# Attention of a first layer: one set of scores with a row-maximum bias, probabilities transposed by DMA, value products in bursts

## What is computed

```python
xn = _layernorm(x, axis=-1)
q = (xn @ Wq)  # 32 heads of 16;  k, v = xn @ Wk, xn @ Wv  # 8 heads of 16, each used by 4 q heads
attn = jnp.einsum('bhqd,bhkd->bhqk', q, k) * scale          # scale = 1/sqrt(16), float16
attn = jax.nn.softmax(attn, axis=-1).astype(jnp.float16)
out = jnp.einsum('bhqk,bhkd->bhqd', attn, v)
s = out @ Wo
g = _silu(_L0_ffn_ref(xn, ...))     # Hadamard transforms, up, gate, down
x = x + s * g                       # then the second layer
```

## Time and profile before

| | us |
|---|---|
| median of the runs | 1365.99 |
| lowest, highest of 3 runs | 1365.13, 1367.12 |
| span of the profiled execution | 1361.7 |
| of it, busy: PE / DVE / ACT / POOL | 1315.0 / 1063.5 / 737.4 / 528.7 |
| row maxima, L621, 512 of them | 329.1 |
| exponentials, L936, 512 of them | 277.1 |
| second scores, L1132, 512 of them | 99.7 |

### The profile page before, as it was taken

How to read it: one execution, slowest core, us unless ns; L and a number is a source line. 1 busy time by engine, 2 the same in 40 slices (tenths; PEclk the granted TensorE clock), 3 DMA queues, 4 the chain that set the end, 5 groups by cost and what they waited for, 6 DMA issues and landing times. The chain is left out here.

```text
span 1361.7 us, 24113 instructions
## 1 busy us (share of the span) xinstructions
PE 1315.0 (97%) x8866; PEld 640.7 (47%) x8866; DVE 1063.5 (78%) x1855; ACT 737.4 (54%) x1307; POOL 528.7 (39%) x434
## 2 busy tenths in 40 slices
PE   5888999999999999999999999999999999999998
PEld 2333333333333333333344546855486555855475
DVE  7888978778877887788884985778776976868846
ACT  5675666556655666556657552455334652355431
POOL 3499953012211221112222763247431762328431
PEclk9998999999999999999999999999999999999999
DMA  6520000010000000000254024002311024001121
GB/s 232 190 81 8 7 9 3 15 41 14 9 17 32 24 7 7 24 30 15 87 196 184 20 52 82 25 24 60 51 44 40 8 71 82 17 32 43 34 46 47
DMA packets 80468, 68.50 MB, mean 50 GB/s; under 512 B 46080, under 2 KB 67296, under 8 KB 77792
## 3 DMA queue, kind: packets, MB, share of 16 engines
q1 hardware_dynamic: 67936, 65.39, 15.5%
q10 hardware_dynamic: 12416, 1.57, 1.1%
HBM read 44.87 MB, written 17.87 MB: 46 GB/s over the span
## 5 line engine op out<-in xcount | busy, mean ns | idle before, releaser
L621 DVE TENSOR_REDUCE mS<-vpair 128x1 f16<-128x512 f32 x512 | 329.1, 685 | 111.6 <-PE vpair L1125 109.5
L936 ACT ACTIVATE probs<-bank 128x512 f16<-128x512 f32 x512 | 277.1, 594 | 163.0 <-PE bank L1132 162.8
L1179 PE MATMUL bank<-rows,both 128*128 128x512 f16 x1024 | 243.0, 380 | 0.4 <-DVE th L650 0.3
L436 POOL TENSOR_TENSOR h<-th,h 128x512 f16<-128x512 f32 x61 | 71.4, 1171 | 213.2 <-ACT h L907 213.2
L1179 PEld LDWEIGHTS bank<-rows,both 128*128 128x128 f16 x1024 | 91.3, 98 | 121.2 <-issue 13.9
L2257 PE MATMUL bank<-rows,both 128*128 128x512 f16 x512 | 118.6, 382 | 0.0
L1125 PE MATMUL vpair<-qk 32*128 32x512 f16 x512 | 100.3, 387 | 13.1 <-DVE mS L621 7.7
L2273 PE MATMUL bank<-both,hid 128*128 128x512 f16 x512 | 111.2, 379 | 0.0
L2241 PE MATMUL bank<-rows,both 128*128 128x512 f16 (+1 forms) x456 | 104.0, 379 | 0.9 <-PEq L160 0.9
L1132 PE MATMUL bank<-qv,qk 32*128 32x512 f16 x512 | 99.7, 386 | 0.0
L1193 PE MATMUL bank<-dn,h 128*128 128x512 f16 x256 | 98.0, 383 | 0.0
(11 more groups left out here) (363 smaller groups left out, 2654.1 us busy)
## 6 DMA issues: line engine op xcount, KB each, us to landing
h<-in_ug SPq DMA_DIRECT2D x8, 1024.0 KB, 5.5
lt_scratch<-big SPq DMA_DIRECT2D x16, 384.0 KB, 2.7
dn<-in_down SPq DMA_DIRECT2D x2, 2048.0 KB, 11.1
x_scratch<-th SPq DMA_DIRECT2D x16, 256.0 KB, 2.2
res<-x_scratch SPq DMA_DIRECT2D x16, 256.0 KB, 4.3
out_x<-res SPq DMA_DIRECT2D x16, 256.0 KB, 2.0
both<-in_w SPq DMA_DIRECT2D x2, 1548.0 KB, 10.4
t_scratch<-tok SPq DMA_DIRECT2D x16, 192.0 KB, 2.1
```

What stands on the lines that cost most here:

```text
L436: pool.tensor_tensor(h16(ft, 1), row32, h16(ft, 0), ALU.subtract).then_inc(S["row_lo"], 1)
L621: v.tensor_reduce(mS[:, u % 2, qt, 32 * j + DH:32 * j + DH + 1], SA[n % 2][:, :], AX.X, ALU.max).then_inc(S["max_done"], 1)
L936: a.activation(probs[:, n % (2 * G), :], SB[n % 2][:, :], ACT.Exp, scale=float(DH) ** -0.5).then_inc(S["p_ready"], 1)
L1179: mm = pe.matmul(GB[n % 2][:, :], w[:, kt, col:col + P], xnb(b, kt), start=r == 0, stop=r == 2 * KT - 1)
```

## The change

Scores are made once, with queries on the partitions, four tiles (four heads of one row tile) at a time into four banks `SC_`, in every second step (`scores`). The row maximum is negated and stays a column in float32 (`top_n`); the exponential takes it as bias and reads the same bank, so the scale goes into q's eviction. The probabilities of a row tile, 128 x 2048, lie in one of three buffers (`TAKEN`). SyncE transposes them by a DMA through the crossbar into `probsT`, keys on the partitions (`turn_probs`, one per two steps, 128 in all), once the four exponentials are there and, since `probsT` is single, once the unit before has been weighed. `weigh` makes a unit's 16 value products in one burst at the third step of the next unit (`PV_STEP`), when all its transposes have landed. `turn_maxima`, `q_aug`, `score_b`, `mS`, `qB` and `onecol` go; GpSimd clears k's padding. On VectorE four maxima stand together in even steps with `up_mul` ahead of them, and `chunk_max` moves a step earlier. Turning back to tokens, division and `to_features` stand 7, 7 and 6 steps earlier.

```diff
+TAKEN = 3
+PV_STEP, TOKEN_STEP, DIVIDE_STEP, TURN_BACK = 2, 3, 4, 6
-        SA, SB, OB, GB, MISC = bank[0:2], bank[2:4], bank[4], bank[5:7], bank[7]
+        SC_, OB, GB, MISC = bank[0:4], bank[4], bank[5:7], bank[7]
...
+        top_n = sb("top_n", [P, 2 * SC], F32)
+        probs = sb("probs", [P, TAKEN, G * T], F16)
+        probsT = sb("probsT", [P, SC, T], F16)
...
+            def turn_probs(n):
+                u, qt = divmod(n, TT)
+                sp.wait_ge(S["p_ready"], G * (n + 1))
+                if u:
+                    sp.wait_ge(S["pv_done"], u)
+                sp.dma_start_transpose(probsT[:, :, qt * P:(qt + 1) * P], probs[:, n % TAKEN, :]).then_inc(S[f"pt_in{n % TAKEN}"], 16)
...
             for t in range(TEND):
                 b, m = t // BSTEPS - 1, t % BSTEPS
+                if t % 2 == 0 and 0 <= t // 2 - 1 < NU * TT:
+                    turn_probs(t // 2 - 1)
...
-            pool.memset(mS[:, :, :, :], 0.0).then_inc(S["init"], 1)
+            pool.memset(ks[:, :, :], 0.0).then_inc(S["slots_set"], 1)
...
             def row_max(n):
+                v.wait_ge(S["s_ps"], n + 1)
+                i = n % (2 * SC)
+                v.tensor_reduce(top_n[:, i:i + 1], SC_[n % G][:, :], AX.X, ALU.max, negate=True).then_inc(S["max_done"], 1)
...
-                if t < NU * STEPS:
-                    row_max(2 * t)
-                    row_max(2 * t + 1)
...
+                if t > FFN_STEP + 1 and (t - 2) // BSTEPS < B and (t - 2) % BSTEPS >= FFN_STEP and t % 2 == 0:
+                    up_mul((t - 2) // BSTEPS, ((t - 2) % BSTEPS - FFN_STEP) // 2)
+                if t < NU * STEPS and t % 2 == 0:
+                    for j in range(G):
+                        row_max(2 * t + j)
...
             def exps(n):
+                a.wait_ge(S["max_done"], n + 1)
+                k, j = divmod(n, G)
+                if j == 0 and k >= TAKEN:
+                    a.wait_ge(S[f"pt_in{k % TAKEN}"], 16 * (k // TAKEN))
+                i = n % (2 * SC)
+                a.activation(probs[:, k % TAKEN, j * T:(j + 1) * T], SC_[j][:, :], ACT.Exp,
+                             bias=top_n[:, i:i + 1]).then_inc(S["p_ready"], 1)
...
+            def scores(n):
+                u, qt = divmod(n, TT)
+                if qt == 0:
                     pe.wait_ge(S[f"heads_in{u % SLOTS}"], 128 * (u // SLOTS + 1))
+                if n:
+                    pe.wait_ge(S["p_ready"], G * n)
+                for j in range(G):
+                    pe.matmul(SC_[j][:, :], qs[32 * j:32 * j + 32, u % SLOTS, qt * P:(qt + 1) * P],
+                              ks[32 * j:32 * j + 32, u % SLOTS, :], start=True, stop=True).then_inc(S["s_ps"], 1)
+
+            def weigh(u):
+                b, g = divmod(u, NKV)
+                for i in range(TAKEN):
+                    pe.wait_ge(S[f"pt_in{i}"], 16 * ((TT * (u + 1) - 1 - i) // TAKEN + 1))
...
+                for kt in range(TT):
+                    for j in range(G):
+                        mm = pe.matmul(OB[32 * j:32 * j + 32, :], vaug[:, b % 2, kt, g, :], probsT[:, TT * j + kt, :],
+                                       start=kt == 0, stop=kt == TT - 1)
...
-                if t < NU * STEPS + LAG:
-                    four_scores(t)
-                if t % STEPS == 0 and 0 < t <= NU * STEPS:
-                    turn_maxima(t // STEPS - 1)
+                if t < NU * STEPS and t % 2 == 0:
+                    scores(t // 2)
+                if t % STEPS == PV_STEP and 0 <= t // STEPS - 1 < NU:
+                    weigh(t // STEPS - 1)
```

More of the change, by code:

```diff
@@ L101, in misc_order @@
         b, m = t // BSTEPS, t % BSTEPS
-        if t % STEPS == 0 and 0 < t <= NU * STEPS:
-            order.append(("mT", t // STEPS - 1))
         if t in TURN_STEP:
@@ L800, in _ @@
                     inverse_deviations(3)
-                if r == 0 and 0 <= p < NCH:
-                    chunk_max(p)
-                    if p == NCH - 1:
-                        bound_inputs()
+                if r == 3 and 0 <= p + 1 < NCH:
+                    chunk_max(p + 1)
+                if r == 0 and p == NCH - 1:
+                    bound_inputs()
                 if t == 29:
@@ L979, in _ @@
             deviations(2)
-            a.wait_ge(S["init"], 4)
+            a.wait_ge(S["init"], 3)
             evict_v(0)
@@ L1111, in project_o @@
                 mm.then_inc(S["mb_full"], 1)
-            def turn_maxima(u):
-                pe.wait_ge(S["mb_took"], MB["mT", u])
-                pe.wait_ge(S["max_done"], (u + 1) * SC)
-                bk = MISC[:, :].bitcast(F16)
-                for qt in range(TT):
-                    mm = pe.transpose(bk[:, qt * P:(qt + 1) * P], mS[:, u % 2, qt, :], ident[:, :])
-                mm.then_inc(S["mb_full"], 1)
-            def score_a(n):
-                u, i = divmod(n, SC)
-                qt, j = divmod(i, G)
-                pe.matmul(SA[n % 2][:, :], qs[32 * j:32 * j + 32, u % SLOTS, qt * P:(qt + 1) * P],
-                          ks[32 * j:32 * j + 32, u % SLOTS, :], start=True, stop=True).then_inc(S["sa_ps"], 1)
@@ L1157, in weigh @@
+            def weigh(u):
                 b, g = divmod(u, NKV)
-                pe.wait_ge(S["p_ready"], G * w + G)
-                if kt == 0 and u:
+                for i in range(TAKEN):
+                    pe.wait_ge(S[f"pt_in{i}"], 16 * ((TT * (u + 1) - 1 - i) // TAKEN + 1))
+                if u:
                     pe.wait_ge(S["o_free"], u)
-                if kt == 0 and g == 0:
+                if g == 0:
                     pe.wait_ge(S["mb_took"], MB["v", b] + 1)
-                for j in range(G):
-                    mm = pe.matmul(OB[32 * j:32 * j + 32, :], vaug[:, b % 2, kt, g, :], probs[:, (G * w + j) % (2 * G), :],
-                                   start=kt == 0, stop=kt == TT - 1)
+                for kt in range(TT):
+                    for j in range(G):
+                        mm = pe.matmul(OB[32 * j:32 * j + 32, :], vaug[:, b % 2, kt, g, :], probsT[:, TT * j + kt, :],
+                                       start=kt == 0, stop=kt == TT - 1)
@@ L2614, in host_layout @@
     o["nhad"] = c(-had.astype(np.float32))
-    one = np.zeros((P, 1), np.float32)
-    one[DH::32] = 1.0
-    o["onecol"] = one
     return o
```

113 lines of the change are left out of this document (28 added, 85 removed).

## The result

| | before | after |
|---|---|---|
| median of the runs, us | 1366.55 | 1482.68 |
| lowest, highest | 1365.13, 1368.22 | 1479.72, 1485.11 |
| ratio, with its 95% interval | | 1.0858 (1.0842 to 1.0874) |
| span of the profiled execution | 1361.7 | 1477.9 |

The kernel became 8.6% slower, where 1375 us (+0.7%) was forecast. The span grew by 116.2 us. I cut both spans at the starts of scores in the timeline, at t = 0, 32, 64 and then each 32 steps. "To scores" is the time to the first scores.

A forecast was written before the change was run, and what follows sets the result against it. The bound was to go from TensorE to the chain of scores, maxima and exponentials. Span 1361.7 + 10.2 + 0.4 - 4 = 1368.3, medians 4.3 higher, plus 2.4 for start loads and x1 transfers: 1375 us (1355 to 1400); range 1340 to 1490.

The forecast's parts named there:

- The wait at the burst: TensorE waits for a unit's fourth transpose: 1.8 us, four times per down half (7.2 us); nothing in feed-forward halves.
- The formula of the wait: Down half: fourth transpose 1.8 us late, plus 4.0 landing and 0.1, less 4.1 until TensorE asks: 1.8 us.
- The issue of a transpose: SyncE's queue: 0.6 us per transpose, as for a plain DMA; 4.7 us if issued by blocks of 16 partitions.
- The halves without waits: First layer's double steps summed without transpose waits: down half 64.4 us (68.2 before), feed-forward half 81.3 (81.2 before).
- The exponential with a column bias: ScalarE's exponentials in the new loop, priced at 0.594 us each as in the kernel before.
- Tanh in the feed-forward chain: ScalarE's high half (0.63 us) and tanh (0.67) stand between exponential pairs, making the plain double step 4.7 us.
- Rival 2: Faster: transposes land in 3.0 us, issue 0.33, tanh perhaps outside the feed-forward loop; 1350 us (1335 to 1360), chance 0.31.
- The start: Steps t < 32: no change, 8 us either way, the same work but for its order.
- The end: After t = 256 nine steps lose their second scores, 0.33 + 0.1 us each: -4 us.
- Rival 1: SyncE's queue is the bound: issue by blocks, 4.7 us, gives 1570 us (1480 at 3.9); TensorE's clock falls; chance 0.22.
- Rivals 3 and 4: 3: transposes write 32 B pieces, over 2500 us, chance 0.03. 4: four scores don't overlap, 1375 to 1385, chance 0.02.

The follow-up runs named there:

- e4: The changed kernel without its 128 transposes and the waits on them, value products reading a constant tile; 1378.62 us, ratio 1.0099.
- e5: The changed kernel with each transpose replaced by a plain DMA of the same 512 KB in pieces of 256 B; 1461.03 us (one run).
- e7: The changed kernel with twelve extra, unused products on TensorE ahead of the burst's wait for the transposes; 1470.77 us, ratio 1.0772.
- e1: The changed kernel with a unit's eight head loads issued behind its fourth transpose, k's projection six steps later; 1388.71 us, ratio 1.0170.
- e8: e4 with the exponentials also taking no bias; 1361.48 us, ratio 0.9969.
- e9: e1 with the value burst one step later and the rows' high half ahead of a double step's first two exponentials; 1364.56 us, ratio 0.9990.
- e12: e9 with a block's four exponentials together at the even step for all t; 1417.72 us, ratio 1.0387.
- e11: e9 with a block's four exponentials together at the even step for t < 32 only; 1371.91 us, ratio 1.0046.
- e10: e9 with the next layer's first four loads issued ahead of the very last transpose; 1372.78 us, ratio 1.0053.

## Why the prediction was wrong

**The wait at the burst and what follows it (the step that failed).** The sum had this wait at 4 x 1.8 us in a down half, at nothing in a feed-forward half ("costs nothing"), and no price for the clock behind it: 21.6 us in all. With e4 as the kernel without transposes, the halves from t = 64 on show (us; the waits are the idle time just ahead of the bursts):

| | after | e4 | more | of it waits | rest | forecast |
|---|---|---|---|---|---|---|
| three down halves | 256.0 | 198.1 | 57.9 | 39.1 | 18.8 | 21.6 |
| three feed-forward halves | 278.4 | 238.9 | 39.5 | 25.1 | 14.4 | 0 |

So the term was 97 us and not 21.6. The mean wait is 3.3 us in a down half and 2.1 in a feed-forward half; the feed-forward halves, forecast at nothing, are the largest single miss. These 76 us are most of the 107 by which the forecast was short; the start and the end, below, are the others.

**The formula of the wait** was right: issue + loads + landing + 0.1, less two double steps. With what the trace shows for the burst at 455.74 it gives 1.93 + 5.7 + 4.33 + 0.1 - 7.9 - 0.33 = 3.8 us, measured 3.60; I had 1.8. Of the 2.0 more, 1.3 are the issue, 0.8 the eight head loads (5.7 for 4.93), 0.3 the landing, less 0.4 since the double steps are longer. In a feed-forward half the same terms give about 2 us, measured 2.31: the margin there was 0.3 us, and a margin as small as that was no reason to put the term at nothing.

**The issue of a transpose** is the input that was furthest off. I took 0.6 us, "since every plain DMA of whatever size is 0.33 to 0.6", and kept 0.33 to 1.2 for the range. It is 1.93. The rows of before had no transpose, and the evidence used was of another kind of DMA; even there 0.33 to 0.6 held for medians only (one load of 1 MB took 1.26). The 4.7 that I named as a rival bounded it from above, and a value between the two was the honest choice. But it is not the whole step: e5, with an issue of 0.65, still takes 1461 us (one run), 86 over the forecast.

**The clock behind the wait.** I had the fall of the clock in rows 7 and charged it to the first rival only. My own forecast had TensorE idle for 1.8 us in 12 bursts with no such charge. What the clock took is read in three ways: 1.2 us per burst of a down half on average by e7, 36.9 us of TensorE's busy time between the changed kernel and e1, and the rest of the table, 33.2, which holds whatever else differs. It does not fall behind every wait: a burst at 522.23 waited for 2.86 us, and the 4.3 us behind it were granted 1.00.

**The halves without waits: right in size.** 64.4 and 81.3 summed, 64.6 and 81.7 measured in e4 (the first down half, with 68.9, and the last feed-forward half, with 75.5, differ, as they did before). But the agreement hides the next error: the exponentials in these sums were too short, and other terms too long by as much (e8, with exponentials of 0.60, has 63.3 and 79.2).

**The exponential with a column bias.** 594 ns was taken from rows 4 for an instruction that got a new operand; it is 687 to 690. That is 17 us over the kernel (e8).

**Tanh in the feed-forward chain.** Rival 2 had it that plain double steps could be 4.4 us if something slipped out of the loop; they are 4.73 in the changed kernel, and 4.2 in e9, by the high half and not by tanh (e12 shows what becomes of tanh outside).

**The start.** "0, 8 us either way" for t < 32; it is +11.6, and +8.8 more for t = 32 to 63. By the first 32 steps: without transposes 112.9, also without bias 108.9, before 105.9. So 4.6 are the transposes and 4.0 the bias; the 3.0 left may be the order of four scores at a time, but no run isolates it. For the second stretch, transposes 0, bias 2.5, and the high half's place most of the rest (97.9 in e9). Why e9's first 32 steps are still 8.4 longer stays open in its parts; putting the pairs together makes it longer (e11).

**The end.** -4 was forecast, it is +8.3. I had counted nine steps without second scores and not what else starts there. The next layer's loads stand behind the last transpose in SyncE's queue: they start 785.74 - 777.5 = 8.2 us after the last scores, where before it was 671.9 - 669.6 = 2.3. In e4, without transposes, it is 684.3 - 680.3 = 4.0, and its end is still 6.3 over before's. So the queue explains a part, and what makes the rest was not isolated.

**Rival 1** ends up at the measured time (1480 at an issue of 3.9 us) by a wrong mechanism. It said that the queue is the bound from 2.9 us on; the issue is 1.93, the queue is not the bound (e1), and the loss is a place in the queue and the clock. Its note on the clock was right. Without that rival's width the range would have ended far below the time: that 1340 to 1490 holds 1482.68 is luck.

**Rivals 3 and 4** fell. The queue has 334032 packets where it had 67936: 2079 more per transpose, so pieces of 256 B and not of 32. And the four scores overlap: the two pairs start 0.01 us apart.

In sum: of the 116 us, e4 puts the transposes' part at 104, or up to 109 without the late first scores of e4; 94 of them went with the place of the fourth one (e1). What they cost in e1 all the same, 10 to 15 us, was not taken apart.

## What to carry to other kernels

Before a DMA is put into a full queue, list for each one what stands ahead of it in that queue and when the consumer asks for it; one late entry behind eight small loads cost 94 us here, and moving the loads behind it gave them back. A term that comes out at nothing by a small margin (0.3 us here) needs a price too. Where a step of a sum makes TensorE wait, add the clock behind the wait (1.2 us per burst on average in a down half here), and where an instruction gets a new operand, don't take its old duration. A loop over banks holds everything that an engine does between its first and last reader: moving one 0.63 us instruction out of it was worth 24.6 us, and moving another one out lengthened a different chain by more.

## What the runs showed of the hardware

- SyncE's issue of a transpose of 128 x 2048 in two-byte values takes 1.93 us, of 128 x 1024 1.33 us, of a plain DMA of the same pieces 0.65 us. The entries behind it in the queue are issued after it.
- Landing from issue: 4.3 us for the 512 KB transpose, 4.2 for the plain copy, 3.2 for a 256 KB transpose. The longest issues of a transpose were 8.6 us in the changed kernel (at 49.1 us) and 11.2 in e10, right behind large loads.
- A column as bias makes ScalarE's 128 x 512 exponential 0.69 us instead of 0.60.
- After a wait of 3.60 us at a burst TensorE ran for some 3.5 us mostly at 1.2 GHz (0.60 granted); with 2.76 us of other products ahead of such waits it was granted 1.00 in all six halves (e7).
